# Graph attention passes: one gathered column per 128-row tile, a larger leftover list, and the node update on ScalarE

## The reference, cut to what matters

```python
def gat_conv(x, src, dst, W, a_src, a_dst, b):
    h = (x @ W).reshape(n, H, D)                       # H = 8 heads of D = 16
    e_src = jnp.sum(h * a_src, axis=-1)
    e_dst = jnp.sum(h * a_dst, axis=-1)
    e = jax.nn.leaky_relu(e_src[src] + e_dst[dst], 0.2)
    m = segment_max(e, dst)
    w = jnp.exp(e - m[dst])
    alpha = w / (segment_sum(w, dst)[dst] + 1e-16)
    return segment_sum(h[src] * alpha[:, :, None], dst).reshape(n, H * D) + b
h1 = gat_conv(x, ..., W1, ...); h2 = gat_conv(h1, ..., W2, ...); h3 = gat_conv(h2, ..., W2, ...)
return jax.nn.log_softmax(h3, axis=1)
```

## Time and profile before

| | us |
|---|---|
| median of 3 runs | 9813.22 (9797.62 to 9823.6) |
| the profiled execution | 9859.25 |
| its span, first to last instruction | 9857.6 |

### The profile page before, as it was taken

The page is one execution under the profiler, slowest core; times in us unless marked ns, Lnnn a source line. Parts: engine busy times, 40 slices in busy tenths (PEclk is TensorE's granted clock), DMA queues, the critical chain, the costliest instruction groups (busy, mean ns, idle before and its releaser), DMA issues. The chain is left out here.

```text
span 9857.6 us, 108932 instructions
## 1 busy us (share of the span) xinstructions
PE 3178.9 (32%) x25103; PEld 2415.9 (25%) x25104; DVE 4758.8 (48%) x12125; ACT 1393.2 (14%) x3116; POOL 4700.7 (48%) x5051
## 2 busy tenths in 40 slices
PE   4241455554444345653456533444000000000000
PEld 3230233332223244553345522333000000000000
DVE  9475344444445444554455555666455444322222
ACT  0210111111111112211112212222111111000000
POOL 0001455554443434543345434454666665666666
PEclk9997555555555566666666666666555555555555
DMA  0121333332232223342233422223222222222212
GB/s 17 32 44 20 68 84 82 82 81 73 71 69 63 52 51 58 61 61 45 53 56 61 58 44 46 45 47 39 49 52 52 48 50 45 42 46 46 47 46 44
DMA packets 337153, 525.00 MB, mean 53 GB/s; under 512 B 191894, under 2 KB 214083, under 8 KB 336971
## 3 DMA queue, kind: packets, MB, share of 16 engines
q0 software_dynamic: 158976, 370.76, 22.3%
q1 hardware_dynamic: 143674, 113.61, 4.0%
q10 hardware_dynamic: 34449, 40.02, 1.3%
HBM read 499.67 MB, written 24.39 MB: 53 GB/s over the span
## 5 line engine op out<-in xcount | busy, mean ns | idle before, releaser
L2316 PE MATMUL bank<-tab,oh 128*128 128x136 bf16 x17082 | 1364.8, 245 | 1543.4 <-PEq L2311 934.9
L2316 PEld LDWEIGHTS bank<-tab,oh 128*128 128x128 bf16 x17082 | 1227.6, 109 | 1694.4 <-issue 1693.3
L2092 POOL DMA_INDIRECT land_a<-table,run_now x825 | 1062.5, 1288 | 302.1 <-issue 244.4
L1859 POOL DMA_INDIRECT land_a<-table,idx_a x936 | 914.9, 977 | 348.2 <-issue 262.2
L1859 POOL DMA_INDIRECT land_b<-table,idx_b x936 | 909.8, 972 | 347.9 <-issue 273.2
L1859 POOL DMA_INDIRECT land_c<-table,idx_c x912 | 903.2, 990 | 334.2 <-issue 242.7
L1321 PE MATMUL bank<-ident,hid 128*128 128x128 f32 x175 | 76.6, 437 | 2127.2 <-issue 1136.5
L1972 PE MATMUL bank<-rel,onehot 64*128 64x128 f32 x1856 | 511.0, 451 | 681.4 <-PEq L1970 498.2
L1972 PEld LDWEIGHTS bank<-rel,onehot 64*128 64x128 f32 x1856 | 449.8, 324 | 1010.0 <-issue 1010.0
L2101 POOL DMA_INDIRECT land_r<-table,idx_r x516 | 498.0, 965 | 225.0 <-issue 157.0
L1321 PEld LDWEIGHTS bank<-ident,hid 128*128 128x128 f32 x175 | 32.9, 188 | 2222.8 <-issue 2221.9
(11 more groups left out here) (397 smaller groups left out, 6573.5 us busy)
## 6 DMA issues: line engine op xcount, KB each, us to landing
loc<-el_loc SPq DMA_DIRECT2D x78, 800.0 KB
typ<-el_typ SPq DMA_DIRECT2D x232, 128.0 KB
attr<-in_edge_attr ACTq DMA_DIRECT2D x75, 343.8 KB
land_a<-table,idx_a POOLq DMA_INDIRECT x936
land_b<-table,idx_b POOLq DMA_INDIRECT x936
land_c<-table,idx_c POOLq DMA_INDIRECT x912
land_a<-table,run_now POOLq DMA_INDIRECT x825
land_r<-table,idx_r POOLq DMA_INDIRECT x516
```

The lines of the kernel that those rows point to most:

```text
L1859: pool.indirect_dma_start(rows_of(x, h, width)[:, n, :], None, source, bass.IndirectOffsetOnAxis(ap=idx[x][:, c:c + 1].bitcast(U32), axis= ...
L2092: pool.indirect_dma_start(land_a[:, c, :], None, source, bass.IndirectOffsetOnAxis(ap=run_now[:, c:c + 1].bitcast(U32), axis=0)).then_inc( ...
L2316: last = pe.matmul(ps_got[g % PSB][:, c * W1:(c + 1) * W1], onehot_of(g, c, k), tab[:, g * GB + k, x], start=n == 0, stop=n == len(parts) ...
```

## The change

It re-tiles the nodes in tiles of 125 (padded to 128) instead of groups of 375: one column per tile, so PC stays 25 but a run takes 75 matmuls. FIRST becomes 13 and MORE 8. By the inputs' edges the blocks then need 3,2,2,2,1,1,1,2 and then 1 turn each, 31 turns in a pass. `land_r` and its copy on ACT are gone: POOL gathers a turn straight into `rows_r`. `take_landed` for the next run moves to the end of the current one, and POOL issues one more `gather_first` behind the last block. In passes 1 and 2 the work of L1335 and L1388 to L1393 moves from DVE to ACT, and the copy of L1348 to POOL. One-hots are one instruction, and `loc` is free right behind it. `rows` is free behind the product. The list stage finds one key per tile with two products of 25 by 64 and one reduction. More small steps compute tile numbers in the early stage.

```diff
-GB = 3
-GC = 3
-FIRST = 11
-MORE = 4
+FIRST = 13
+MORE = 8
+BANKC = 3
...
-                        for g in range(NGR):
-                            dve.scalar_tensor_tensor(below[:, g], keys[0][:, 0:RUN], float((g + 1) * GR * RUN + 1), keys[0][:, 0:RUN],
-                                                     ALU.is_lt, ALU.mult).then_inc(ch.semaphore, ch.one())
-                        dve.wait_ge(ch.semaphore, ch.count)
-                        for g in range(NGR):
-                            dve.max(best[:, g], below[:, g]).then_inc(ch.semaphore, ch.one())
-                        dve.max(best[:, NGR], keys[0][:, 0:RUN]).then_inc(ch.semaphore, ch.one())
...
+                        of_run = keys[0][:, 0:RUN].unsqueeze(1).broadcast_to([P, NB, RUN])
+                        dve.tensor_tensor(below[:], of_run, end_of[:].unsqueeze(2).broadcast_to([P, NB, RUN]), ALU.is_lt).then_inc(ch.semaphore, ch.one())
+                        dve.wait_ge(ch.semaphore, ch.count)
+                        dve.tensor_tensor(below[:], below[:], of_run, ALU.mult).then_inc(ch.semaphore, ch.one())
+                        dve.wait_ge(ch.semaphore, ch.count)
+                        dve.tensor_reduce(best[:], below[:], AX.X, ALU.max).then_inc(ch.semaphore, ch.one())
...
-                    dve_to_conv(dve, ch, b, wait, n + 2, meanwhile)
+                    dve.sem_inc(s("hid_ready"), 1)
                     return
...
+        def act_to_conv(act, b, before_this):
...
+            act.wait_ge(s("hid_turned"), 1)
+            act.sem_inc(s("hid_turned"), -1)
+            act.activation(hid_t[:], ps_t[:, 0:P], ACT.Copy).then_inc(s("act_chain"), 1)
+            done()
+            act.sem_inc(s("hid_t_ready"), 1)
+            act.sem_inc(s("hid_free"), 1)
+            act.wait_ge(s("table_stored"), 16 * (before_this - 1) + 16 * (b + 1))
+            act.wait_ge(s("projected"), 1)
+            act.sem_inc(s("projected"), -1)
+            act.activation(stage1[:, 0:D], ps_p[:, 0:D], ACT.Copy)
+            act.activation(stage1[:, D:W1], ps_p[:, D:W1], ACT.Identity, bias=padneg[:, bass.ds(b, 1)]).then_inc(s("act_chain"), 1)
+            done()
+            act.sem_inc(s("table_ready"), 1)
+            act.activation(blk(own1, b, 0, D + REC), ps_p[:, 0:D + REC], ACT.Copy).then_inc(s("act_chain"), 1)
+            done()
...
                             with pool.Fori(0, turns) as i:
-                                pool.wait_ge(s("land_r_free"), 1)
-                                pool.sem_inc(s("land_r_free"), -1)
+                                pool.wait_ge(s("rows_r_free"), 1)
+                                pool.sem_inc(s("rows_r_free"), -1)
...
                                 for c in range(MORE):
-                                    pool.indirect_dma_start(land_r[:, c, :], None, source,
+                                    pool.indirect_dma_start(rows_r[:, c, :], None, source,
...
                     with pool.Fori(1, NB) as b:
                         gathers(b)
-                        scatter(pool, stage, target)
-                    scatter(pool, stage, target)
+                        store_rows(b - 1, 16 * (before_this - 1) + 16 * b)
+                    gather_first()
+                    store_rows(NB - 1, 16 * (before_this + NB - 1))
...
-                        for k in range(GB):
-                            dve.tensor_scalar(oh[:, k * OHW:(k + 1) * OHW], loc[:, 0:OHW], iota_k[:, k:k + 1], None, ALU.is_equal).then_inc(s("oh_ready"), 1)
-                        dve.tensor_scalar(oh[:, GB * OHW:], loc[:, OHW:], iota_k[:, 0:1], None, ALU.is_equal).then_inc(s("oh_ready"), 1)
+                        dve.tensor_scalar(oh[:].rearrange("p c n -> p (c n)"), loc[:], iota_p[:], None, ALU.is_equal).then_inc(ch.semaphore, ch.one())
+                        dve.wait_ge(ch.semaphore, ch.count)
+                        dve.sem_inc(s("oh_ready"), 1)
+                        dve.sem_inc(s("loc_free"), 1)
...
                         with act.Fori(r0, r1) as r:
...
-                            take_landed(r)
                             exps(0)
-                            rows_wanted()
-                            take_rows(range(PSB))
-                            with act.Fori(0, turns) as i:
-                                act.wait_ge(s(f"got_r{number}"), (t0 + i) * (16 * MORE) + 16 * MORE)
-                                act.wait_ge(s("rows_r_free"), 1)
-                                act.sem_inc(s("rows_r_free"), -1)
-                                act.activation(rows_r[:], land_r[:], ACT.Copy).then_inc(s("act_chain"), 1)
-                                copied("land_r_free", "rows_r_in")
+                            take_rows()
+                            with act.Fori(0, turns):
                                 exps(MC - MORE)
-                            take_rows(range(PSB, NGR + 1))
...
+                            take_landed(r + 1)
...
                             for c in range(m):
-                                parts = [(k, x) for k in range(sizes[g]) for x in range(3)]
-                                for n, (k, x) in enumerate(parts):
-                                    last = pe.matmul(ps_got[g % PSB][:, c * W1:(c + 1) * W1], onehot_of(g, c, k), tab[:, g * GB + k, x],
-                                                     start=n == 0, stop=n == len(parts) - 1, skip_group_check=True)
+                                for x in range(3):
+                                    last = pe.matmul(ps_got[g % PSB][:, c * W1:(c + 1) * W1], oh[:, g * BANKC + c], tab[:, g * BANKC + c, x],
+                                                     start=x == 0, stop=x == 2, skip_group_check=True)
```

More of the change, by code:

```diff
@@ L95, in program @@
     SCALE = 1.0 / HD ** 0.5
[L96 to L99, removed]
+    GN, PADS = N // NB, P - N // NB
+    FIVE = 5
+    assert N == NB * GN and PADS > 0 and NB == FIVE * FIVE
+    PC = NB
     MC = PC + FIRST
@@ L2077, in _, with gather_first @@
                     ch = Chain(s("pool_chain"))
+                    def gather_first():
+                        pool.wait_ge(s("list_in"), 16)
+                        pool.sem_inc(s("list_in"), -16)
+                        pool.wait_ge(s("land_a_free"), 1)
+                        pool.sem_inc(s("land_a_free"), -1)
+                        pool.tensor_copy(run_now[:], run_idx[:]).then_inc(ch.semaphore, ch.one())
+                        pool.wait_ge(ch.semaphore, ch.count)
+                        pool.sem_inc(ch.semaphore, -ch.clear())
+                        pool.sem_inc(s("list_free"), 1)
+                        for c in range(FIRST):
+                            pool.indirect_dma_start(land_a[:, c, :], None, source,
+                                                    bass.IndirectOffsetOnAxis(ap=run_now[:, c:c + 1].bitcast(U32), axis=0)).then_inc(s(f"got_a{number}"), 16)
                     def gathers(b):
@@ L2194, in chunks @@
                             weigh(b, rows[:], 0, MC, "rows_free", onehots)
-                            with dve.Fori(0, turns):
-                                dve.wait_ge(s("rows_r_in"), 1)
-                                dve.sem_inc(s("rows_r_in"), -1)
+                            t0 = dve.value_load(rstart[0:1, bass.ds(r, 1)], min_val=0, max_val=RMAX * RUN // MORE)
+                            with dve.Fori(0, turns) as i:
+                                dve.wait_ge(s(f"got_r{number}"), (t0 + i) * (16 * MORE) + 16 * MORE)
                                 weigh(b, rows_r[:], MC - MORE, MORE, "rows_r_free")
-                    for name in ["land_a_free", "land_r_free", "rows_free", "rows_r_free"]:
+                    for name in ["land_a_free", "rows_free", "rows_r_free"]:
                         dve.sem_inc(s(name), 1)
+                    if not by_dve:
+                        dve.sem_inc(s("hid_free"), 1)
                     onehots()
```

216 lines of the change are left out of this document (106 added, 110 removed).

## The result

| | before | after |
|---|---|---|
| median, same call (13 runs each) | 9807.3 us | 9839.23 us |
| ratio after / before | | 1.0027 (95% interval 1.0015 to 1.0039) |
| span of the profiled execution | 9857.6 us | 9831.6 us |

The change makes the kernel slower by 0.27%; the medians are 32 us apart, about the 29 us that I had called the least that can be told. I had forecast 1.2% faster: the sign is wrong. The time (9839 against 9690) lies inside my range of 9440 to 9980, but only because the range was wide enough to hold the other outcomes too.

What follows compares the result with a forecast made beforehand. PE's late matmuls, then ACT's queue, set the block. From the profiled 9859.25 us: passes -66 -71 -106, pass ends +49, starts -12, list stage +80, early stage +5, sum -121; 9690 us at the median, range 9440 to 9980.

Steps and rivals of the forecast that it cites:

- 2.1 us from the scatter to the first gather: One-turn block, POOL: scatter, copy of the list and start of the first gather take 2.1 us.
- 6.1 us of held gathers: One-turn block: DVE's work beside the 13 gathers adds 4.5 us for the product and an estimated 1.6 for the rest.
- my own break-even: One-turn block length at which the change gains nothing: 42.6 us, against the 40.5 forecast.
- The 3.8 us of the earlier trace: Kernel before: mean hold over 825 first gathers, 3.8 us a block of 11; preferred to some 9 by the port rule.
- `hid_free` and the `table_stored` waits: at nothing: Waits on ACT and POOL that the change adds: priced at nothing, as their events are a block old.
- My bound from below: One-turn block if POOL alone sets it: 21 x 1.25 + 2.1 + 1.0 + 6.1 = 35.5 us.
- Pass 3: Blocks 2 us less than in passes 1 and 2, 38.5 and 62; the pass 1055.5 against 1161.1 us, -106.
- Two-turn blocks of passes 1 and 2: Second turn waits for the one buffer, +23.5 to 64.0 us; third turn +16; passes 1 and 2 gain -66 and -71.
- List stage: Two products and a reduction replace 2.48 us: +3.2 us a run, 25 runs, +80; from below 62, from above 112.
- ACT is held under the turn stream: Slower rival, chance 0.32: POOL's 8 turn gathers hold ACT or PE; blocks 45 us (9950) half held, 51.5 (some 10320) fully.
- G + 15.5: One-turn block: table ready 15.5 us after G, the end of the 13th first gather, through landing and ACT's work.
- The faster rival: POOL's rounds cheaper, ACT's 9.0 us shrink, bound falls to POOL's 35.5: 9405 us, 9520 at 37.5; chance 0.13.

Runs made afterwards that it cites:

- the high level: Calls where the unedited kernel before took 9807 us, or 9986 to 9991 in two; changed kernel's ratio there 1.0027 and, run again, 1.0002.
- the two kernels above: Changed kernel without edit, and with the node update of passes 1 and 2 back on DVE: low-level ratios 1.0506 against 1.0314 and 1.0318.
- the low level: Five later calls where the unedited kernel before took 9062 to 9093 us; the unedited changed kernel took 9520, ratio 1.0506.
- with 147 of them: Kernel before with groups of two tiles, 147 matmuls a run, FIRST 12: ratio 0.9757 at high level; 1.0020, 1.0023, 1.0009 at low.
- the second: Changed kernel run again without edit, in a later high-level call: 9983.5 us, ratio 1.0002 to the kernel before.
- two edits that take ACT's order off the path: Changed kernel with exponentials early and the three feature loads behind the node update, both on ACT: 9734 us, ratio 0.9743, high level.

## Why the prediction was wrong

**The step that failed: the POOL terms of the one-turn block, 2.1 us from the scatter to the first gather and 6.1 us of held gathers.** Both kernels of the result ran in one call, at the high level, so the levels don't explain the miss. My block was 15.5 + 2.1 + 16.2 + 6.1 + 0.6 = 40.5. Over the one-turn blocks of passes 1 and 2 POOL's timeline gives 15.2 for the first term, 3.45 for the second, 15.9 for the 13 gathers and 7.3 for what holds them: 41.9, and 42.2 from weighing to weighing. The chain over ACT to the scatter was right; what POOL does behind it was mis-sized by 1.3 and 1.2 us. The 2.1 came from a row behind a scatter that POOL had not waited for. 38 blocks make +65 us. In pass 3 it was worse, 41.4 and not 38.5, 19 blocks, +55 us. Together that is 120 us, all that I had forecast to gain. It is 2.1 us a block, my own break-even.

What held gathers cost stood in the kernel before. These are further first gathers of the block of the earlier trace rows, whose 5.42 is in the earlier trace rows (POOL's timeline, before):

```profile
3810.72 1.28 POOL L2092 DMA_INDIRECT land_a<-table,run_now  x1 [0.30 <-issue]
3812.30 1.55 POOL L2092 DMA_INDIRECT land_a<-table,run_now  x1 [0.30 <-issue]
...
3821.14 2.23 POOL L2092 DMA_INDIRECT land_a<-table,run_now  x1 [0.30 <-issue]
```

The 11 first gathers of such a block are held 7.0 us in sum. Those that run beside the weighing of a block with several turns are hardly held, 0 to 0.4 us in pass 1. The 3.8 us of the earlier trace rows is the mean of the two kinds, and I used it against a larger price in the very block where it doesn't hold. The change turned six of the multi-turn blocks of a pass into the dear kind. The 6.1 us of my sum had an estimated 1.6 for everything beside the product.

**The other terms**, in the call of the prediction:
- "`hid_free` and the `table_stored` waits: at nothing". The copy of `stage_i` and the wait of `store_rows` cost 2.1 us a block where POOL is the bound: 0.8 in front of the scatter, 1.3 behind it, by the two kernels above. My bound from below, POOL alone at 35.5, was 3.6 us too low: these 2.1 and the longer holds.
- Pass 3: I had taken 2 us off because the features are gone, without a row. The scatter does come 1.5 us sooner, 13.7 us behind G. But the same 1.3 us stands behind it, and DVE's one-hots, product and halving all lie beside the first gathers (POOL, one block of pass 3):

```profile
6011.39 0.24 POOL L2103 COPY run_now<-run_idx 128x72 int32<-128x72 int32 x1 [1.33 <-POOLq L2102]
...
6015.65 5.97 POOL L2108 DMA_INDIRECT land_a<-table,run_now  x1 [0.31 <-issue]
6021.93 3.38 POOL L2108 DMA_INDIRECT land_a<-table,run_now  x1 [0.30 <-issue]
```

  Its first gathers are held 8.4 us. Two-turn blocks were 66.7 and not 62, the three-turn block 82.8 and not 76: pass 3 missed by +80 us in all, the largest single miss.
- Two-turn blocks of passes 1 and 2: 64 forecast, 65.4 measured, and three turns 80 forecast, 70.5 measured. That the gain comes from the multi-turn blocks was right: in pass 1 the eleven of before gained 54 us, and the other thirteen lost 19. The ends of passes: +12.4 and +15.8, forecast +12 each; behind the last pass +4.5, forecast +16.
- List stage: +80 forecast, +61.5 measured; the durations were right (1.82, 1.83, 1.82), the loop hid part of them.
- The shared port: the sum had product and halvings at 6.1 us where 7.3 and, in pass 3, 8.4 were held. The Trainium skill's rule on the port that VectorE and GpSimd share ("SBUF — State Buffer", "SBUF: two separate sides") pointed that way: by that rule, the trace of after agrees for the product, 5.63 us beside 5.23, and over the block it comes nearer to the 9 us worked out from it than to 3.8.

**What the levels add.** I took 7.12 us of waiting for PE and 6.10 for ACT, in a block of 41 us, for the kernel's own. The same code takes 32 to 33 us at the low level, where a block has 0.68 and 4.13 of them. So most of what the change removes, PE's stalls and DVE's wait for them, exists only at the high level, where it about pays for the longer work on POOL; at the low level the change costs 5%. That PE's late matmuls set the block was right in part: with 147 of them about half of the added wait is still there.

**The rivals.** "ACT is held under the turn stream" is in part what the high level shows: the loads are issued 3.5 us late, POOL idles for ACT's rows in front of the scatter for 2.9 us a block in the first call and 4.7 in the second, the blocks are 42.2 and 43.6, and two edits that take ACT's order off the path give 39.6. My G + 15.5 already held that delay: at the low level the scatter comes at G + 12.9. The faster rival, POOL's sum as the bound, came true as a bound at the low level, at 39.1 (the shortest blocks) and not 35.5.

**What stays open.** What makes the two levels. That at the high level PE, ACT's issues and DVE's waits are slow together while POOL gathers, and recover within 1.4 to 2.4 us of its last gather, is what the rows show. The gathers themselves are not slower there (1288 ns in the mean against 1282 at the low level), and the granted clock is not the cause; no run here separates a short supply of instructions from late semaphores. Whether the node update is better on DVE at the high level has not been run.

## What to carry to other kernels

Before costing a stall from one profile, run the unchanged kernel again in another call, and see whether the stall is there: here 740 us of 9800 came with the call. Where a change hands work to the engine that issues gathers, count every copy, wait and loop head on its queue, not the gathers alone, and look where the long operations that hold it will fall in the new order. A mean over blocks of two kinds prices neither: 3.8 us of held gathers in the mean were 7.0 in one kind and nearly nothing in the other.

## What the runs showed of the hardware

- The same kernel, 9062 to 9093 us in five calls and 9807 to 9991 in three; within a call the runs agree to 0.8%, at either granted clock (0.61 and 0.73, or 0.60 and 0.71).
- The first gathers of a block are held by DVE's long operations beside them: 7.0 us in a one-turn block of the kernel before, 7.3 in the changed one, 8.4 in its pass 3. The gather that starts with the product is as long as it, 5.63 us beside 5.23.
- At the high level ACT's issue of the same loads stretches beside POOL's gathers. In the changed kernel the node copy follows ACT's copy of the landed rows by 11.6 us (3894.98 to 3906.53); at the low level, with the same order and gathers, by 7.9:

```profile
3810.69 1.68 ACT L2272 ACTIVATE rows<-land_a 128x1768 f32<-128x1768 f32 x1 [10.21 <-DMA land_a<-table,run_now]
...
3818.56 0.28 ACT L1468 ACTIVATE hid_t<-bank 128x128 f32<-128x128 f32 x1 [2.60 <-ACTq L1467]
```

- The level is not one of the attention passes only: behind the last main weighing the kernel before takes 3003 us in the first call and 2852 at the low level, the changed one 3008 in the first call, 3086 in the second at the high level and 2861 at the low one.
